# A graph layer's edges, sorted on the chip into blocks of one pair of node tiles

## What is computed

```
x   = layernorm(x)                          # 625 x 256
xl  = x @ W_l;  xr = x @ W_r                # 4 heads of 64
e   = xl[src] + xr[dst]                     # one row per edge
e   = where(e >= 0, e, 0.2 * e)
score = einsum('ehd,hd->eh', e, att)        # 4 numbers per edge
ex  = exp(score - max over the edges of dst)
agg = segment_sum(ex / denom[dst] * xl[src], dst)
```

## Time and profile before

| | us |
|---|---|
| Runs | 1161.45, 1166.17, 1166.57; median 1166.17 |
| Span of the profiled execution | 1154.3 |
| Busy: PE / DVE / ACT / POOL | 948.9 / 858.0 / 466.5 / 463.7 |
| First scatter starts | 70.1 |
| Last scatter starts, lands | 515.86, 518.4 |

### The profile page before, as it was taken

The page is one execution under the profiler, slowest core; times in us unless marked ns, Lnnn a source line. Parts: engine busy times, 40 slices in busy tenths (PEclk is TensorE's granted clock), DMA queues, the critical chain, the costliest instruction groups (busy, mean ns, idle before and its releaser), DMA issues.

```text
span 1154.3 us, 19240 instructions
## 1 busy us (share of the span) xinstructions
PE 948.9 (82%) x6532; PEld 829.5 (72%) x6532; DVE 858.0 (74%) x1953; ACT 466.5 (40%) x795; POOL 463.7 (40%) x374
## 2 busy tenths in 40 slices
PE   4586998879989998983835999985898588599996
PEld 2566886768978887853734999974588377589885
DVE  5659468869777978997987888776688765866635
ACT  1453755467858686616621111110253053212120
POOL 2448888877777877860001222250000000211104
PEclk9888999789999999997865999997999698699999
DMA  8962222323222232209704999983000000588883
GB/s 295 276 194 64 56 69 68 74 48 73 63 62 62 63 77 47 48 11 247 189 1 137 324 316 333 316 299 116 0 1 1 1 1 1 211 307 304 297 317 91
DMA packets 57946, 157.58 MB, mean 137 GB/s; under 512 B 23797, under 2 KB 32938, under 8 KB 49618
## 3 DMA queue, kind: packets, MB, share of 16 engines
q1 hardware_dynamic: 26830, 125.59, 33.3%
q0 software_dynamic: 25056, 24.10, 9.3%
q10 hardware_dynamic: 5992, 7.04, 1.7%
HBM read 136.50 MB, written 19.86 MB: 135 GB/s over the span
## 4 chain that ended last, share of the span: by engine, by line
PE 33%; DMA 24%; DVE 17%; POOL 12%; issue 10%; SPq 3%; POOLq 0%; ACT 0%; DVEq 0%; ACTq 0%
DMA pair_scores<-sc_ring,idx_ring 13%; PE bank L775 11%; PE bank L786 6%; POOL pair_scores L2153 5%; POOL arena L2143 5%; DMA arena<-pair_scores 4%; PE bank L544 3%; PE bank L708 2%; POOL arena L2208 2%; PE bank L496 2%; SPq L2232 2%; DMA arena<-slot_y,sloti 2%; DMA arena<-in_exp 1%; PE bank L697 1%; PE bank L874 1%
## 5 line engine op out<-in xcount | busy, mean ns | idle before, releaser
L2198 POOL DMA_INDIRECT arena<-row_tab,ids x42 | 57.7, 1373 | 493.7 <-DVE ids L1563 486.6
L2153 POOL DMA_INDIRECT pair_scores<-sc_ring,idx_ring x160 | 210.2, 1314 | 60.3 <-issue 43.4
L2143 POOL DMA_INDIRECT arena<-xl_tab,idx_ring x120 | 157.6, 1313 | 81.3 <-issue 31.7
L775 PE MATMUL bank<-arena 128*128 128x128 f32 x1480 | 180.8, 280 | 3.2 <-DMA arena<-in_exp 3.0
L775 PEld LDWEIGHTS bank<-arena 128*128 128x128 f32 x1480 | 175.0, 197 | 5.3 <-DMA arena<-in_exp 4.1
L1888 ACT ACTIVATE arena<-fmaps,node_neg 125x875 f32<-125x875 int32 x100 | 100.1, 1022 | 34.5 <-PE bank L544 34.5
L786 PE MATMUL bank<-arena 128*128 128x256 f32 (+1 forms) x404 | 97.6, 384 | 1.2 <-DMA arena<-in_exp0o 1.2
L1892 ACT ACTIVATE late_ohT<-arena 125x875 fp32r<-125x875 f32 x100 | 90.6, 926 | 0.0
L2021 ACT ACTIVATE arena<-bank 128x512 f32<-128x512 f32 (+2 forms) x76 | 34.4, 453 | 126.6 <-PE bank L775 126.5
L544 PE MATMUL bank<-late_hi,late_ohT 125*125 125x256 f32 x500 | 83.7, 298 | 0.6 <-DVE arena L1035 0.6
L786 PEld LDWEIGHTS bank<-arena 128*128 128x128 f32 (+1 forms) x404 | 72.1, 190 | 14.9 <-issue 6.0
(11 more groups left out here) (357 smaller groups left out, 2017.4 us busy)
## 6 DMA issues: line engine op xcount, KB each, us to landing
arena<-in_exp SPq DMA_DIRECT2D x25, 1024.0 KB, 7.1
arena<-in_exp SPq DMA_DIRECT2D x17, 1386.0 KB, 6.1
arena<-in_exp0o SPq DMA_DIRECT2D x25, 512.0 KB, 7.3
pair_scores<-cnt SPq DMA_DIRECT2D x10, 1093.8 KB
arena<-in_exp1o SPq DMA_DIRECT2D x17, 640.0 KB
fmaps<-in_rows SPq DMA_DIRECT2D x20, 437.5 KB, 3.8
arena<-pair_scores SPq DMA_DIRECT2D x7, 1093.8 KB
slot_y<-arena ACTq DMA_DIRECT2D x34, 128.0 KB, 6.4
```

The costliest lines, as they stand in the source:

```text
L775: mm = pe.matmul(banks[1 + 2 * q + buf][0:rows, i * SLOTS:(i + 1) * SLOTS], w_in(s, q, k, m, rows), xsT[:, s, k, :], start=(k == 0), stop= ...
L2143: p.indirect_dma_start(out=gat[:, b % 2, 0, j * D:(j + 1) * D], out_offset=None, in_=xl_tab, in_offset=bass.IndirectOffsetOnAxis(ap=idx_ri ...
L2153: p.indirect_dma_start(out=pair_scores[which], in_=sc_ring[:, b % 2, j, :], in_offset=None, out_offset=bass.IndirectOffsetOnAxis(ap=idx_ri ...
L2198: p.indirect_dma_start(out=xs[:, q, :], out_offset=None, in_=tab, in_offset=bass.IndirectOffsetOnAxis(ap=ids[:, q, :], axis=0))\
```

## The change

Only the part up to the dense attention changes. The edges are first sorted on the chip.

- **Sorting.** A node's tile is `id // 125`; with five tiles there are 25 buckets (dst tile, src tile). Each bucket gets as many columns of 125 slots as it needs; at most `SORTED = 184` columns arise, 92 pairs (`PAIRS`). VectorE computes each edge's bucket and 25 masks, TensorE counts and sums them (`sum_members`, `sum_columns`, `begin_blocks`, `owners`, `slots`), and VectorE derives each edge's slot (`find_slots`). Then, for each of the 160 edge columns, two bf16 matmuls of 184 columns put the local node numbers into their slots (`sort_edges`): VectorE makes the place masks (`choose_places`), GpSimd the column masks of three columns in four (`find_column`), ScalarE of the fourth (`find_columns`). Empty slots hold 0 and are written to spare cells behind the table.
- **A pair.** All edges of a column now have one dst tile and one src tile. VectorE makes four bf16 masks of 125 (`make_hots`). TensorE turns them and counts with a 125 x 125 product (`turn_hots`), ScalarE copies the turned masks (`copy_hots`), and TensorE sums both rows from the one tile they need, at an address that it reads into registers (`sum_rows`, four values per pair): eight matmuls of 260 columns, 256 and the four head sums of `0.6 * att * row`. ScalarE takes `0.4 * |z|` (`read_rows`), VectorE multiplies by att and reduces (`score`); it adds each column's counts to `cnt` at a register address (`add_counts`, eight values read every fourth pair). On each engine the pair's row sums stand ahead of the next pair's turning.
- **Transfers.** There are no gathers, no table of xl in HBM and no spread edge lists. 184 scatters remain, alternately to the two tables, each waiting for the previous one to its table. The edge lists are loaded first of all, then x, then two constant arrays.
- **The mixer** is dealt out to pairs 6 to 40 by the table `MIX`, and has three banks. All these loops are unrolled.

The core of the diff:

```diff
+BUCKETS = T * T
+SORTED = (E + BUCKETS * (P - 1)) // P
+PAIRS = SORTED // 2
+TAKEN = 3
+CHOSEN = 6
+HOTS = 3
+SCORED = 16
+MIX_BANKS = 3
+ROW = D + H
+SUM_BANKS = (6, 7, 3)
+MIX = {"ln1": 6, "mixh": 8, "turned": 10, "xm": 11, "qkv_in": 12, "softened": 14, "turned_kq": 15, "kv": 17, "qkv": 18,
+       "attn": 20, "ln2": 22, "h2": 23, "h2T": 25, "m1": 26, "m2": 35, "added": 40}
...
-            def rows_of(g, s, late, r):
-                columns = PIECES[r]
-                if r == 0:
-                    pe.wait_ge(sem("rows_hot"), g + 1)
-                after(pe, sem("z_read"), g * NP + (r + 1 - NP))
-                for i, j in enumerate(columns):
-                    terms = [(part, j) for part in xr_parts]
-                    if late and columns == MADE:
-                        terms += [(part, G + i) for part in xl_parts]
-                    for n, (part, at) in enumerate(terms):
-                        for t in range(T):
-                            mm = pe.matmul(banks[T + r][0:P, i * D:(i + 1) * D],
-                                           hot[late, s][:, t, at * P:(at + 1) * P], part[:, t, :],
-                                           start=(n == 0 and t == 0), stop=(n == len(terms) - 1 and t == T - 1))
-                mm.then_inc(sem("z_made"), 1)
...
+            def slots():
+                for i, b in enumerate(range(0, BUCKETS, 3)):
+                    after(pe, sem("slots_read"), i - 1)
+                    for q in range(b, min(b + 3, BUCKETS)):
+                        to = banks[3 + i % 2][0:P, (q - b) * EC:(q - b + 1) * EC]
+                        pe.matmul(to, before[:, :], member[:, q, :], start=True, stop=False)
+                        mm = pe.matmul(to, orders[:, q * P:(q + 1) * P], slots_before, start=False, stop=True)
+                    mm.then_inc(sem("slots"), 1)
+            def sort_edges():
+                for j in range(EC):
+                    pe.wait_ge(sem("chosen"), j + 1)
+                    if j % 4 == 3:
+                        pe.wait_ge(sem("act_columns"), j // 4 + 1)
+                    else:
+                        pe.wait_ge(sem("pool_columns"), j // 4 * 3 + j % 4 + 1)
+                    for w in range(2):
+                        mm = pe.matmul(banks[5 + w][0:P, 0:SORTED], chosen[:, j % CHOSEN, w, :],
+                                       columns16[:, j % CHOSEN, :], start=(j == 0), stop=(j == EC - 1))
+                    mm.then_inc(sem("placed"), 1)
+            def turn_hots(c):
+                pe.wait_ge(sem("onehot"), c + 1)
+                after(pe, sem("counted"), c - 1)
+                bank = banks[4 + c % 2]
+                to_d, to_s = (onehot[:, c // 2 % TAKEN, c % 2, w, :] for w in range(2))
+                pe.matmul(bank[0:P, 0:P], to_d, ident16[:, :], start=True, stop=True)
+                pe.matmul(bank[0:P, P:2 * P], to_s, ident16[:, :], start=True, stop=True)
+                pe.matmul(bank[0:P, 2 * P:3 * P], to_d, to_s, start=True, stop=True).then_inc(sem("turned_hots"), 1)
+            def sum_rows(i):
+                _, rows = nc.values_load_multi_w_load_instructions(
+                    at_rows[0:1, 2 * i:2 * i + 2, :].rearrange("p c w -> p (c w)"), engines=[mybir.EngineType.PE],
+                    min_val=0, max_val=(2 * T - 1) * ROW)
+                for c in range(2):
+                    pe.wait_ge(sem("hot"), 2 * i + c + 1)
+                    after(pe, sem("z_read"), 2 * i + c - 2)
+                    n = 0
+                    for w in range(2):
+                        for part in (hi_rows, lo_rows):
+                            mm = pe.matmul(banks[SUM_BANKS[(2 * i + c) % 3]][0:P, 0:ROW], hot[0:P, i % HOTS, c, w, :],
+                                           part[:, bass.ds(rows[2 * c + w], ROW)], start=(n == 0), stop=(n == 3))
+                            n += 1
+                    mm.then_inc(sem("z_made"), 1)
...
+            linear_tm("lr", fa, lambda k: W("lr", k), 2 * D)
+            sort_edges()
+            read_out(pe, "lr")
+            ring["n"] = MIX_BANKS
+            pe.wait_ge(sem("sorting"), SORTING["ident16"])
+            pe.wait_ge(sem("parts"), T + 3)
+            pe.wait_ge(sem("sorting"), SORTING["owners_read"])
+            pe.wait_ge(sem("sorting"), SORTING["nodes_read"])
+            turn_hots(0)
+            turn_hots(1)
+            for i in range(PAIRS):
+                sum_rows(i)
+                for c in (2 * i + 2, 2 * i + 3):
+                    if c < SORTED:
+                        turn_hots(c)
+                mix(i)
+            pe.wait_ge(sem("hot"), SORTED)
+            pe.wait_ge(sem("counted"), SORTED)
+            pe.wait_ge(sem("z_read"), SORTED)
...
+            def find_buckets():
+                dve.wait_ge(sem("edges_in"), 32 * len(PARTS))
+                own.link(v.tensor_copy(nodes_f, edge_ids[:, :, :]))
+                own.link(v.tensor_scalar(digits, nodes_f, float(P), None, ALU.is_ge))
+                for k in range(2, T):
+                    own.link(v.scalar_tensor_tensor(digits, nodes_f, float(k * P), digits, ALU.is_ge, ALU.add))
+                own.note(v.scalar_tensor_tensor(local, digits, -float(P), nodes_f, ALU.mult, ALU.add))
+                own.link(v.scalar_tensor_tensor(bucket, digits[:, 1, :], float(T), digits[:, 0, :], ALU.mult, ALU.add))
+                for b in range(BUCKETS):
+                    ins = v.tensor_scalar(member[:, b, :], bucket, float(b), None, ALU.is_equal)
...
+            def choose_places():
+                for j in range(EC):
+                    after(dve, sem("placed"), j - CHOSEN + 1)
                     for w in range(2):
+                        ins = v.tensor_scalar(chosen[:, j % CHOSEN, w, :], iota_c[:, 0:P], place_of[:, j:j + 1],
+                                              local[:, 1 - w, j:j + 1], ALU.is_equal, ALU.mult)
+                    ins.then_inc(sem("chosen"), 1)
...
+            def make_hots(i):
+                after(dve, sem("turned_hots"), 2 * (i - TAKEN + 1))
+                for c in range(2):
+                    for w in range(2):
+                        ins = v.tensor_scalar(onehot[:, i % TAKEN, c, w, :], iota_1[:, :],
+                                              node_at[:, w, 2 * i + c:2 * i + c + 1], None, ALU.is_equal)
+                    ins.then_inc(sem("onehot"), 1)
+            def add_counts(i):
+                if i == 0:
+                    dve.wait_ge(sem("cnt_zero"), 1)
+                if i % 4 == 0:
+                    n = min(8, SORTED - 2 * i)
+                    _, regs = nc.values_load_multi_w_load_instructions(
+                        at_counts[0:1, 2 * i:2 * i + n], engines=[mybir.EngineType.DVE], min_val=0, max_val=T * N - P)
+                    count_at[:] = regs
+                for c in (2 * i, 2 * i + 1):
+                    dve.wait_ge(sem("hot"), c + 1)
+                    after(dve, sem("counted"), c)
+                    to = cnt_flat[:, bass.ds(count_at[c % 8], P)]
+                    v.tensor_tensor(to, to, banks[4 + c % 2][0:P, 2 * P:3 * P], ALU.add).then_inc(sem("counted"), 1)
+            count_at = []
+            def score(i):
+                rows = weighed[:, i % 2, :, :, :]
+                dve.wait_ge(sem("z_read"), 2 * i + 2)
+                for c in range(2):
+                    ins = v.tensor_tensor(rows[:, c, :, 0:HD], rows[:, c, :, 0:HD],
+                                          Vt(0, "att").rearrange("p (h d) -> p h d", h=H), ALU.mult)
+                    own.note(ins)
...
+                own.fence()
+                v.tensor_reduce(sc_ring[:, i % SCORED, :, :].rearrange("p c h -> p (c h)"),
+                                rows.rearrange("p c h d -> p (c h) d"), AX.X, ALU.add).then_inc(sem("scored"), 1)
...
+            copy_sums()
+            count_blocks()
+            begin_slots()
+            copy_owners()
+            dve.wait_ge(sem("x_in"), 16 * len(PARTS))
+            layernorm(x, xn, 1e-5, (sem("xn"), T))
+            find_slots()
+            dve.wait_ge(sem("ident"), 2)
+            v.tensor_copy(ident16[:, :], ident[0:P, 0:P]).then_inc(sem("sorting"), 1)
+            from_fm("xnT0", fa)
+            choose_places()
+            split_rows()
+            read_nodes()
+            make_hots(0)
+            make_hots(1)
+            find_cells()
+            add_counts(0)
+            for i in range(PAIRS):
+                if i + 2 < PAIRS:
+                    make_hots(i + 2)
+                if i + 1 < PAIRS:
+                    add_counts(i + 1)
+                score(i)
+                mix(i)
+            dve.wait_ge(sem("counted"), SORTED)
...
+            def copy_hots(c):
+                act.wait_ge(sem("turned_hots"), c + 1)
+                after(act, sem("z_made"), 2 * (c // 2 - HOTS + 1))
+                a.activation(hot[0:P, c // 2 % HOTS, c % 2, :, :].rearrange("p w n -> p (w n)"),
+                             banks[4 + c % 2][0:P, 0:2 * P], ACT.Copy).then_inc(sem("hot"), 1)
```

(30 more changed lines are left out.)

1012 lines of the change are left out of this document (415 added, 597 removed).

## The result

| | before | after |
|---|---|---|
| Median of four runs, us | 1164.11 | 1214.47 |
| Lowest, highest | 1161.45, 1166.57 | 1209.48, 1220.94 |
| Span of the profiled execution | 1154.3 | 1215.0 |

After over before is 1.0446, 95% interval 1.0399 to 1.0493: slower by 4.5%, where 1.6% was forecast. 1214.47 lies inside the stated range. The sign is right, the size is not.

A forecast was written before the change was run, and what follows sets the result against it. Bound shared by GpSimd and TensorE, the end set by the last scatter's landing: 151 us start + 41 x 3.1 + 75 mixer = 353, + 51 x 3.55 + 2.5 = 537 against 518.4; span 1173, plus 11.9, 1185 us; range 1115 to 1230.

The forecast's parts named there:

- (d): Slots at the start: ten transposes and 50 matmuls at 12 us, then a VectorE reduction of 4.2, ending at 49.5 us.
- (f): Sort of 160 columns: VectorE's masks 58 us, 75 with GpSimd stalls, bounds 58 and 102, ending at 135 us.
- (a) to (c): Start up to the layernorm's end: bucket and membership masks to 13.5 us, counts to 22, layernorm to 28.4.
- (e): x products before the sort, starting once VectorE empties the bank of transposes: 10.84 us, ending at 60 us.
- Rival 3: Slower: the sort is serial and takes 102 us, +27 more, 1212 us; chance 0.12.
- (g): Between sort and first scatter: splitting rows, cells, eight masks, first counts with register read, 16 us, ending at 151.
- A pair on VectorE: Pair loop: VectorE's masks, count additions, products, reduction and register reads sum to 3.1 us per pair (2.8 to 3.4).
- GpSimd at 3.55 us per pair: Last 51 pairs: each scatter waits for the previous one to its table, so GpSimd needs 3.55 us per pair, 181 us.
- rival 1: Faster: GpSimd is bound by issue, 3.08 us per pair, no stall in the sort; -39, 1127 us; chance 0.27.
- The mixer, 75 us: Mixer work between pairs 6 and 40 adds 75 us (60 to 90) beyond the pairs' 3.1 us each.
- Not hidden at the end: Mixer work delays the edge work on the same queue, while GpSimd drains its ring and waits; the 75 us show.
- rival 2: Slower: register reads hold up hand-overs between TensorE, ScalarE and VectorE; a pair takes 4.2 us, +82, 1248 us; chance 0.17.

## Where the prediction was right and wrong

What failed is the price of the start: the forecast had the first scatter at 151 us and it came at 190.3, which is the whole of the 39 us, while the two misses behind it cancel. The mechanism (a sort ahead of everything, then GpSimd's scatters at the end) was right; terms (d) and (f) of the sum were sized too small.

- **What bounds the kernel before, and that the end is the last scatter.** The end is right: the stage behind it moved by 3.5 us of 638, and every experiment's span ends 635 to 644 us behind its last scatter. That GpSimd, and not TensorE, sets the edges before was not tried: every experiment is on the kernel after.
- **(a) to (c).** Within 2.1 us in sum.
- **(d), slots: +18.3 us, the largest miss.** The 50 matmuls were costed at 12 us between bounds of 9 and 18, and took 29, at full clock. The failed step is the price of a short fp32 product with its weight load: 0.82 us per bucket where the bound allowed about half. The reduction over 4000 elements was put at 4.2 and takes 6.83 (1.7 ns per element, where one of 520 has 1.3).
- **(e).** The products took 11.2 us as in the earlier trace rows, but they follow the slots; with a ring of six columns VectorE's waiting time of 8.3 us fell into the sort.
- **(f), the sort: +13.0 with (e).** The nearest row was the wrong one. A GpSimd operation of 0.30 us was taken for a column mask, which costs 0.73 alone, and so GpSimd sets the sort, not VectorE. VectorE's masks, with two scalar operands, stand 0.22 us apart and not 0.18; the stall of some 0.15 us per GpSimd mask and TensorE's 0.33 us per column at half clock (0.31 measured) were right. With these VectorE alone would have needed 2.2 us per four columns, 90 us in all, not 75. Rival 3 has the right size (102, measured 97) and the wrong reason.
- **(g): +5.9.** The first scatter had been put at 150 to 156.
- **A pair on VectorE.** 3.1 forecast, 3.39 measured. Without the checks behind the read it is 2.83, so the rest of the sum was good and the read was sized at half (0.25 against 0.5 us per pair).
- **GpSimd at 3.55 us per pair from the distance of two scatters to one table.** The mechanism holds, and rival 1 with it falls. The size was short by a little: 195 us for the last 51 pairs, not 181. Most distances are 3.4 to 3.6 us; 4 us of the excess are the neighbouring spare cells, and the rest late landings of 4.3 to 5.5 us, whose cause was not tried.
- **The mixer, 75 us.** Too dear: VectorE's 362 us from the first to the last reduction less 91 x 3.39 leave 54. Of the 21 us too many, the dearer pairs took back 12; and the sum counted 41 pairs from the first scatter to pair 40's, where there are 40. Together 14 us less than forecast.
- **Not hidden at the end.** Right: pair 40's scores are there at 377, and GpSimd ends 22 us after VectorE's last reduction.
- **The sum.** The forecast span was 1173 and the measured one 1215.0. To the median it was 1185 against 1214.5, since 11.9 us had been added that belonged to the profiled execution of before (a low one): every run after takes 1.7 to 1.8 us more than its own span, and the median after lies at the profiled span.
- **The range** held the time, by the bounds it took from a serial sort. It would not have reached the kernel with the other order, 1266.83 us, nor was it meant to: rival 2 was left out of it.

## What to carry to other kernels

A sort on the chip is a chain of short stages on a path that nothing covers: each engine's price for its own form of instruction (a GpSimd mask, an fp32 product with its weight load, a checked register read) must come from a row of that form, since the nearest row was short by a factor of two three times here. Where two engines stand side by side (2.28 and 2.2 us here), moving work from the longer gives only the distance to the next; and whether TensorE is full is read from its weight loads' waits, not from its busy time. A wait that looks idle in a fast order can be the one that decides in another: turning one pair of calls round cost over 50 us (1266.83 against 1206.88 to 1220.94).

## What the runs showed of the hardware

- The arithmetic and comparison behind a register read cost more than the load: 8 x 0.206 us against 0.60 on VectorE, and VectorE stands still for it.
- GpSimd's mask of 184 elements takes 0.73 us alone and 0.76 beside VectorE's masks; VectorE loses some 0.15 us by each. A blank of 125 x 3125 fp32 elements on GpSimd held VectorE's masks up for its whole 2.71 us.
- TensorE's granted clock was 0.50 in the sort from 90 us on, after 0.90 from 71 to 90 us (mostly the x products). At 0.50 bf16 matmuls of 184 columns started 0.15 us apart when their masks were there, and 0.26 us apart when weight loads waited for VectorE.
- Scatters of 125 times 16 bytes, each waiting for the previous one to its table, stand 3.75 to 4.29 us apart when they go to neighbouring cells, and 3.31 to 3.47 when the cells lie 512 bytes apart.
